# Key products and half of the value products of the third attention issued at the end of the expert stage before it

## The chip, the cores and the metric

The kernel runs on one core of one Trainium2 chip. The metric is the device time of one execution in microseconds (us). Five engines work from their own instruction queues and meet through semaphores: TensorE (PE; its weight loads are PEld), VectorE (DVE), ScalarE (ACT), GpSimd (POOL) and SyncE (SP), which issues most DMAs.

## The reference, cut to what matters

Four layers follow each other on a residual stream x of 16 x 64 tokens of 256 features; each adds a gated attention over a context and a gated feed-forward part. The change is at the border of the second layer's feed-forward part (eight experts, top 1) and the third layer's attention ("L2" in the reference, "a2" in the kernel):

```python
x = x + tanh(g_ffn[1]) * L1_ffn(layernorm(x), router_w, gate_w, up_w, down_w)
x = x + tanh(g_xattn[2]) * L2_xattn(layernorm(x), ctx_2048, mask, Wq, bq, Wk, bk, Wv, bv, Wo, qn_w, kn_w)
# L2_xattn: 16 query heads, 4 key/value heads, 128 features each
q = rmsnorm(h @ Wq + bq, qn_w);  k = rmsnorm(ctx @ Wk + bk, kn_w);  v = ctx @ Wv + bv
out = softmax(q @ k.T / sqrt(128) + mask) @ v;  x_add = out @ Wo
```

The keys and values come from the context, which is an input. They depend on nothing that the layers before compute.

## The kernel before, in words

Everything stays on the chip from the first load to the last store. The stages run one after the other: `m1_*` are the sorted experts, `a2_*` the attention after them, `m2_*` the next experts. Each engine has one function for each stage. At the end of a stage `finish(e, k)` raises `stage_done` and waits until all four compute engines have done so; SP waits for the same count before the loads of the next stage.

**Experts (`m1`).** The 1024 tokens are sorted by expert into 15 tiles. PE goes through the tiles (line 1724 is its last instruction, a small matmul that marks the end). DVE copies each output tile, SP stores it (line 1648), and then `a2_ahead` loads the key, value and query weights of the attention (lines 1952 and 1953) over the place of the expert weights. After all 15 tiles are stored, POOL gathers the rows back (line 1880) in token order, DVE adds them to x (line 1867), and the stage ends.

**Attention (`a2`).** DVE computes the layer norm of x. PE turns the context tokens and then the normed tokens (`tokens_turned`, line 1971, 16 transposes each), ACT copies them from PSUM (line 2099) over two tiles that the program names `ctxT_yT_hi` and `ctxT_yT_lo`. Then come slots n = -7 to 39, which every engine goes through in the same written order. The 8 tiles of tokens are called pairs (two batches in one tile); a pair takes four slots, and each pair has two units w of eight heads. In a slot PE has, in this order and as far as they fall due:

- the scores of unit w (line 1984, n = 2w), the transposes of probabilities (line 1992, n = 2w + 3), and heads times values (`heads_out`, line 2004, n = 2w + 5)
- the transposes of normed keys (`keys_turned`, line 2013, n = 4i - 1)
- the key product of pair i (`key_or_value(i, 0)`, line 2027, n = 4i - 3) or the value product (`key_or_value(i, 1)`, n = 4i + 3), both into PSUM bank 4, 128x512 in f32: two calls that the trace shows as four instructions
- sums of query squares (line 2059) together with the output product (line 2065)
- the next query product (`queries`, line 2037), into bank 6

The keys of a pair go through DVE (`keys_biased`, line 2193, adds the bias from PSUM), ACT (squares, line 2130), DVE (sums, lines 2199 and 2200), POOL (power of minus a half, line 2259), DVE (`keys_normed`, line 2207) and back to PE (line 2013) within two slots. `queries` on DVE (line 2163) frees bank 6 for the next query product. `outT` on DVE (line 2185) copies what `heads_out` made, as two copies of 128x512. After the last unit DVE makes the layer norm of tiles 0 to 6 (`ln_tiles`) and only then the last residual (line 2222).

The two lines on which all order rests are

```python
e.wait_ge(stage_done, 4 * k)
for n in A2_SLOTS:
```

Of the kernel before, what the change touches and what calls it, by code (L numbers as in the profile page):

```python
# [18 lines left out]
F32 = mybir.dt.float32  # L19
# [61 lines left out]
def program(nc, a):  # L81

    ctx = ExitStack()
    with ctx:
# [197 lines left out]
        def setup_pool(e):  # L282
# [3 lines left out]
        A2_TOTALS = dict(weights_loaded=48, wo_loaded=16, tables_loaded=80, tokens_in_psum=8, tokens_ready=8,  # L286
                         q_in_psum=32, q_squared=32, q_read=0, q_ready=32, squares_in_psum=32, squares_read=8, q_rstd_ready=8,
                         k_in_psum=8, k_squared=8, k_read=8, k_sums_ready=8, k_rstd_ready=8, k_normed=8, kT_in_psum=8, kT_ready=8,
                         v_in_psum=8, v_ready=8, scores_in_psum=16, scores_read=16, max_ready=16, exp_ready=16, sums_ready=16, probs_ready=16,
# [1361 lines left out]
        def m1_pe(e):  # L1651
# [72 lines left out]
            finish(e, 5, e.matmul(ps[:, 0, 0:1], identb[:, :], identb[:, 0:1], start=True, stop=True))  # L1724

        def m1_act(e):
# [39 lines left out]
            finish(e, 5)  # L1766
# [128 lines left out]
        m = Map(nc, ARENA, END - 24 * 1024)  # L1895
        a2wo = m("a2_wo", [P, HQ, D], F32)
        a2kt = m("a2_kT", [P, 2, HK, P], F32)
        a2v = m("a2_v", [P, 2, HK, HD], F32)
# [9 lines left out]
        a2row = m("a2_bias_rows", [P, 2, 512], F32)  # L1908
# [9 lines left out]
        def a2_over(name, shape, dt, offset):  # L1918
            return nc.alloc_sbuf_tensor_at("a2_" + name, shape, dt, offset=offset)
        a2wkv = a2_over("wk_wv", [P, 2, KC, HK * HD], F32, END - 24 * 1024)  # L1920
        a2wq = a2_over("wq", [P, KC, HQ * HD], F32, END - 16 * 1024)
        a2tok = [t[:, :, :, :].rearrange("p r k n -> p (r k n)").bitcast(F32).rearrange("p (r n) -> p r n", r=2) for t in (YCh, YCl)]

        a2_w, a2_wo, a2_in = a2_sem("weights_loaded"), a2_sem("wo_loaded"), a2_sem("tables_loaded")
# [23 lines left out]
        def a2_ahead(e):  # L1948

            e.wait_ge(*m1_dn.at(TILES))  # L1950
            for r, name in enumerate(("a2_wk", "a2_wv")):
                e.dma_start(a2wkv[:, r, :, :], a[name].rearrange("(c p) n -> p c n", p=P)).then_inc(a2_w.sem, 16)
            e.dma_start(a2wq[:, :, :], a["a2_wq"].rearrange("(c p) n -> p c n", p=P)).then_inc(a2_w.sem, 16)

        def a2_sync(e):
            e.wait_ge(stage_done, 20)
            e.dma_start(a2c[:, 0:20], a["a2_cols"]).then_inc(a2_in.sem, 16)
            for r, name in enumerate(("a2_bk", "a2_bv")):
                e.dma_start(a2row[:, r, :], a[name].unsqueeze(0).broadcast_to([P, 512])).then_inc(a2_in.sem, 16)
# [3 lines left out]

        def a2_pe(e):
            def tokens_turned(src, r):
                for b in range(4):
                    cc, th = b % 2, b // 2
                    for j in range(4):
# [1038 lines left out]
```

## Time and profile before

| what | value |
|---|---|
| three runs | 1503.03, 1507.39, 1508.20 us (median 1507.39) |
| the profiled execution | 1499.09 us, its span 1497.3 us |
| PE busy over the span | 1205.3 us (81%) |
| DVE, ACT, POOL busy | 867.8, 607.0, 323.5 us |
| mean granted TensorE clock | 0.873 of full speed |
| PE idle between experts and attention | 603.10 to 618.85 us |
| attention, first query product to end | 629.60 to 867.3 us |

The profiled execution is one run of the program, and all times of engines are from its span's start. A granted clock of 1.00 is 2.4 GHz and one of 0.50 is 1.2 GHz; a number between is a mean over a stretch. An engine's idle time matters only where nothing else holds the end.

### The profile page before, as it was taken

The page shows a single profiled execution, that of the slowest core. Times are in us where ns is not written, and L with a number is a line of the kernel's source. Part 1 is how long each engine was busy: PE and PEld are TensorE (multiplying, and loading weights), DVE is VectorE, ACT ScalarE, POOL GpSimd, SP SyncE. Part 2 cuts the span into 40 slices and gives each one's busy share as a digit, 9 for nine tenths or more (in the row PEclk, how much of TensorE's full clock was granted, in tenths as well). Part 3 has the DMA queues.
Part 4 walks back from the last instruction along what each step waited for, and adds up shares of the span by engine and source line. Part 5 has one row for each costly group of instructions (what it writes and reads, how often), then busy time and mean ns, then how long its engine had stood idle before and what let it go on. Part 6 is the DMA issues. An engine that isn't in the chain of part 4 may idle for free.

```text
span 1497.3 us, 23300 instructions
## 1 busy us (share of the span) xinstructions
PE 1205.3 (81%) x8532; PEld 858.6 (57%) x8577; DVE 867.8 (58%) x1843; ACT 607.0 (41%) x1323; POOL 323.5 (22%) x261
## 2 busy tenths in 40 slices
PE   1573674888885499489999936999997899999986
PEld 1352453444433266488888733555556688888854
DVE  6678795677774463334544575333335776656476
ACT  2441351555563131133333222433333665656443
POOL 1312001111100100221221102445440332222322
PEclk7555796799995699799999957999997999999998
DMA  7100006100002220500000051111103000000010
GB/s 237 51 2 1 0 1 265 65 2 2 2 1 102 81 78 36 195 1 1 1 1 1 1 182 32 43 53 42 42 0 119 0 1 1 1 1 1 1 43 28
DMA packets 32307, 64.31 MB, mean 43 GB/s; under 512 B 5361, under 2 KB 23281, under 8 KB 30289
## 3 DMA queue, kind: packets, MB, share of 16 engines
q1 hardware_dynamic: 31440, 60.90, 11.4%
q0 software_dynamic: 768, 2.10, 0.4%
q8 instruction: 62, 1.02, 0.3%
q14 instruction: 37, 0.30, 0.1%
HBM read 55.26 MB, written 9.70 MB: 43 GB/s over the span
## 4 chain that ended last, share of the span: by engine, by line
PE 50%; issue 19%; DVE 14%; POOL 4%; ACT 3%; DMA 1%; DVEq 0%; SPq 0%; POOLq 0%; ACTq 0%
PE psum L1401 8%; PE psum L1383 4%; PE psum L2420 4%; PE psum L2448 4%; PE psum L2410 4%; PE psum L2392 2%; PE psum L2374 2%; PE psum L1069 2%; PE psum L1043 2%; PE psum L2746 2%; PE psum L1011 1%; PE psum L1076 1%; POOL a_q_rstd L2265 1%; DVE ln_stats L163 1%; PE psum L2037 1%
## 5 line engine op out<-in xcount | busy, mean ns | idle before, releaser
L1468 DVE TENSOR_TENSOR m_silu_up<-psum,m_silu 128x512 f32<-128x512 f32 x50 | 34.6, 691 | 133.3 <-PE psum L1401 133.3
L1135 ACT ACTIVATE c_probs<-psum 128x512 f32<-128x512 f32 x128 | 76.3, 598 | 66.0 <-PE psum L1054 66.0
L1239 DVE TENSOR_REDUCE c_max<-psum 128x2 f32<-128x512 f32 x128 | 84.4, 687 | 27.0 <-PE psum L1043 20.5
L1401 PE MATMUL psum<-ctxT_yT_hi,m_w_lo 128*128 128x512 bf16 x200 | 76.5, 382 | 8.5 <-DVEq L1460 7.2
L1401 PE MATMUL psum<-ctxT_yT_lo,m_w_hi 128*128 128x512 bf16 x200 | 76.3, 382 | 0.0
L2448 PE MATMUL psum<-a_wo,a_outT 128*128 128x256 f32 x256 | 75.1, 405 | 0.7 <-DVE x_tok L2629 0.7
L1496 POOL TENSOR_TENSOR m_h_lo<-m_h,m_h_hi 128x512 bf16<-128x512 f32 x50 | 57.9, 1158 | 82.0 <-ACT m_h_hi L1440 82.0
L2065 PE MATMUL psum<-a_wo,a_outT 128*128 128x256 f32 x256 | 75.2, 407 | 0.0
L1440 ACT ACTIVATE m_h_hi<-m_h 128x512 bf16<-128x512 f32 x50 | 31.5, 630 | 90.5 <-DVE m_h L1473 90.5
L1401 PE MATMUL psum<-ctxT_yT_hi,m_w_hi 128*128 128x512 bf16 x175 | 66.8, 382 | 0.0
L1252 POOL TENSOR_TENSOR c_rope_terms<-c_rope_terms 128x256 f32<-128x256 f32 x16 | 11.6, 726 | 254.3 <-DVE c_rope_terms L1195 254.3
L2163 DVE TENSOR_TENSOR a_qT<-psum,a_columns 128x512 f32<-128x512 f32 x32 | 22.0, 689 | 75.3 <-PE psum L2037 75.3
L1353 POOL TENSOR_TENSOR m_w_lo<-m_w,m_w_hi 128x768 bf16<-128x768 f32 x27 | 44.4, 1646 | 85.1 <-ACT m_w_hi L1347 85.1
L2123 ACT ACTIVATE a_probs<-a_probs,a_max 128x64 f32<-128x64 f32 x128 | 42.7, 334 | 47.3 <-DVE a_max L2177 47.3
L2420 PE MATMUL psum<-ctxT_yT_hi,a_wq 128*128 128x128 f32 x256 | 53.0, 290 | 7.7 <-DVE a_q_cos L2585 7.0
L1689 PE MATMUL psum<-m_w,m_tileT 128*128 x120 | 56.9, 619 | 2.3 <-DVE m_tileT L1844 2.3
L2571 DVE TENSOR_REDUCE a_max<-psum 128x4 f32<-128x512 f32 x32 | 22.1, 691 | 63.2 <-PE psum L2374 63.0
L2488 ACT ACTIVATE a_q_squares<-psum 128x512 f32<-128x512 f32 x32 | 19.1, 598 | 93.9 <-PE psum L2420 93.9
L2512 ACT ACTIVATE a_probs<-psum,a_max,a_q_rstd 128x128 f32<-128x128 f32 x128 | 56.8, 459 | 0.1
L2105 ACT ACTIVATE a_q_squares<-a_qT 128x512 f32<-128x512 f32 x32 | 20.1, 629 | 87.8 <-DVE a_qT L2163 87.5
L1433 ACT ACTIVATE m_silu<-psum 128x512 f32<-128x512 f32 x50 | 29.8, 596 | 62.3 <-PE psum L1401 62.3
L1383 PE MATMUL psum<-m_w_hi,m_h_hi 128*128 128x256 bf16 x200 | 54.5, 272 | 0.6 <-POOL m_h_lo L1496 0.6
(482 smaller groups left out, 3513.5 us busy)
## 6 DMA issues: line engine op xcount, KB each, us to landing
m_w<-m_w SPq DMA_DIRECT2D x8, 1536.0 KB, 17.1
m_w<-m_w SPq DMA_DIRECT2D x27, 384.0 KB, 3.0
a_wq<-a_wq SPq DMA_DIRECT2D x2, 2048.0 KB
a_wo<-a_wo SPq DMA_DIRECT2D x2, 2048.0 KB, 12.5
a_trig<-trig_sin_cos SPq DMA_DIRECT2D x1, 2048.0 KB, 6.2
ctxT_yT_hi<-f_gate_up SPq DMA_DIRECT2D x2, 1024.0 KB, 6.6
a_sin_cos<-a_trig SPq DMA_DIRECT2D x1, 2048.0 KB, 10.1
m_rows<-m_zeros SPq DMA_DIRECT2D x1, 1920.0 KB, 13.9
```

The costliest lines, as they stand in the source:

```text
L1135: e.activation(c1P[:, n % 8, :, :], ps[:, 2 + n % 2, :].rearrange("p (k t) -> p k t", k=2), ACT.Exp, scale=float(1.0 / np.sqrt(np.float32( ...
L1239: e.tensor_reduce(c1M[:, u % 2, j, :], ps[:, c1_score_bank(n), :].rearrange("p (q t) -> p q t", q=2), AX.X, ALU.max).then_inc(c1_mx, 1)
L1353: e.tensor_tensor(wl[:, s, :], wr[:, s, :], wh[:, s, :], ALU.subtract).then_inc(s_wl, 1)
L1383: ins = e.matmul(o, l[:, b, t], r[:, s, 2 * D:3 * D], start=(first and i % 2 == 0 and x == 0), stop=False, skip_group_check=True)
L1401: ins = e.matmul(ps[:, bank, :], l[:, s, o + kc * P:o + (kc + 1) * P], r[:, kc, tk], start=(x == 0), stop=(x == 3 * KC - 1))
L1496: e.tensor_tensor(hl[:, n_ % hb, :], hf[:, n_ % hb, :], hh[:, n_ % hb, :], ALU.subtract).then_inc(s_hl, 1)
L1689: ins = e.matmul(ps[:, 1 + 2 * r + t % 2, :], m1xT[:, t % 2, kc, :], m1w[:, bass.ds(own + (2 * r + kc) * 512, 512)], start=(kc == 0), stop ...
L2065: ins = e.matmul(ps[:, 7, 0:D], a2at[:, i % 2, h, :, :], a2wo[:, h, :], start=(h == 0 and g is None), stop=(h == HQ - 1), skip_group_check ...
L2410: ins = e.matmul(ps[:, 4 + r, :], a3tok[kk][:, b, :, :], a3wkv[:, r, kk, :], start=(kk == 0), stop=(kk == KC - 1))
L2420: ins = e.matmul(out[:, :, h, :], a3wq[:, kk, (4 * j + h) * HD:(4 * j + h + 1) * HD], a3tok[kk][:, 2 * i:2 * i + 2, 1, :], start=(kk == 0) ...
L2448: ins = e.matmul(ps[:, 7, 0:D], a3at[:, i % 2, h, :, :], a3wo[:, h, :], start=(h == 0 and g is None), stop=(h == HQ - 1), skip_group_check ...
L2512: ins = e.activation(a3sc[:, u % 3, p_ * P:(p_ + 1) * P], ps[:, u % 2, p_ * P:(p_ + 1) * P], ACT.Exp, bias=a3mx[:, u % 3, p_:p_ + 1], scal ...
```

## The change

The turning of the context tokens, all eight key products and the value products of pairs 0 to 3 are taken out of the slots. PE and ACT do them at the end of their `m1` functions, after they have raised `stage_done` and before they wait for the others. ACT now copies the products from PSUM without the bias, to two new tiles, `a2_k_raw` and a value tile for all eight pairs. The key bias is added by DVE from that copy. The value bias is no longer added to the values; `outT` adds it (a row of probabilities sums to one) as four operations of 128x256 in place of two copies. The value products of pairs 4 to 7 stay in their slots. The loads keep their place in SP's queue; one bias row less is loaded.

```diff
-        def finish(eng, k, last=None):
+        def done(eng, last=None):
...
             eng.sem_inc(stage_done, 1)
+
+        def finish(eng, k, last=None):
+
+            done(eng, last)
             eng.wait_ge(stage_done, 4 * k)
...
-            finish(e, 5, e.matmul(ps[:, 0, 0:1], identb[:, :], identb[:, 0:1], start=True, stop=True))
+            done(e, e.matmul(ps[:, 0, 0:1], identb[:, :], identb[:, 0:1], start=True, stop=True))
+            context_pe(e)
+            e.wait_ge(stage_done, 20)
...
-            finish(e, 5)
+            done(e)
+            e.wait_ge(f3_q, 3)
+            context_act(e)
+            e.wait_ge(stage_done, 20)
...
+        def a2_context_pe(e):
+            a2_tokens_turned(e, ct, 0)
+            e.wait_ge(*a2_x.at(4))
+            e.wait_ge(*a2_kvw.at(32))
+            for x in range(NT + A2_EARLY_V):
+                i, r = x % NT, x // NT
+                if x >= 4:
+                    e.wait_ge(a2_cr, x - 3)
+                for kk in range(KC):
+                    ins = e.matmul(ps[:, x % 4, :], a2tok[kk][:, 0, i * P:(i + 1) * P], a2wkv[:, r, kk, :], start=(kk == 0), stop=(kk == KC - 1))
+                ins.then_inc(a2_kp.sem, 1)
+
+        def a2_context_act(e):
+            a2_tokens_copied(e, 0)
+            for x in range(NT + A2_EARLY_V):
+                i, r = x % NT, x // NT
+                own = a2v[:, i, :, :].rearrange("p j d -> p (j d)") if r else a2kw[:, i, :]
+                e.wait_ge(*a2_kp.at(x + 1))
+                e.activation(own, ps[:, x % 4, :], ACT.Copy).then_inc(a2_cr, 1)
...
-            tokens_turned(ct, 0)
-            tokens_turned(yt, 1)
+            a2_tokens_turned(e, yt, 1)
             e.wait_ge(*a2_x.at(8))
-            e.wait_ge(*a2_w.at(48))
+            e.wait_ge(*a2_w.at(16))
+            e.wait_ge(a2_cr, NT + A2_EARLY_V)
...
-                if a2_pair(n, 3) is not None:
-                    key_or_value(a2_pair(n, 3), 0)
-                if a2_pair(n, -3) is not None:
-                    key_or_value(a2_pair(n, -3), 1)
+                if a2_pair(n, -3) is not None and a2_pair(n, -3) >= A2_EARLY_V:
+                    value(a2_pair(n, -3))
...
                 for b2 in range(2):
-                    ins = e.tensor_copy(a2at[:, i % 2, 8 * hb:8 * hb + 8, b2, :], ps[:, 1 + 2 * b2, :].rearrange("p (h t) -> p h t", h=8))
+                    for j in range(2):
+                        h = 8 * hb + 4 * j
+                        ins = e.tensor_scalar(a2at[:, i % 2, h:h + 4, b2, :],
+                                              ps[:, 1 + 2 * b2, j * 256:(j + 1) * 256].rearrange("p (h t) -> p h t", h=4),
+                                              a2c[:, 20 + 2 * hb + j:21 + 2 * hb + j], None, ALU.add)
...
-                e.tensor_tensor(a2kf[:, :], ps[:, 4, :], a2row[:, 0, :], ALU.add).then_inc(a2_kr.sem, 1)
+                e.tensor_tensor(a2kf[:, :], a2kw[:, i, :], a2row[:, :], ALU.add).then_inc(a2_kr.sem, 1)
```

Where the instructions stand now. PE at the border of the two stages, before: the last down product of the experts, the marker, the context and the normed tokens turned, then the first query product.

```order
L1707 MATMUL psum<-m_w,m_hT 128x256
L1724 MATMUL psum<-ident_bf 128x1
L1971 MATMUL psum<-ident_f,ctx_tok 128x128 x16
L1971 MATMUL psum<-ident_f,y_tok 128x128 x16
L2037 MATMUL psum<-ctxT_yT_hi,a_wq 128x2x64
```

The same place of PE in the changed kernel; the pair of rows of line 2000 stands there twelve times.

```order
L1712 MATMUL psum<-m_w,m_hT 128x256
L1729 MATMUL psum<-ident_bf 128x1
L1982 MATMUL psum<-ident_f,ctx_tok 128x128 x16
L2000 MATMUL psum<-a_wk_wv,ctxT_yT_hi 128x512
L2000 MATMUL psum<-a_wk_wv,ctxT_yT_lo 128x512
...
L1982 MATMUL psum<-ident_f,y_tok 128x128 x16
L2069 MATMUL psum<-ctxT_yT_hi,a_wq 128x2x64
```

The twelve products have moved ahead of the transposes of the normed tokens, and the context's transposes ahead of the barrier. ACT at the same border, before: the last two copies of turned expert rows, then the copies of turned tokens, four for the context and four for the normed tokens.

```order
L1754 ACTIVATE m_hT<-psum 128x512 x2
L2099 ACTIVATE ctxT_yT_hi<-psum 128x512
L2099 ACTIVATE ctxT_yT_lo<-psum 128x512
L2099 ACTIVATE ctxT_yT_hi<-psum 128x512
L2099 ACTIVATE ctxT_yT_lo<-psum 128x512
L2099 ACTIVATE ctxT_yT_hi<-psum 128x512
L2099 ACTIVATE ctxT_yT_lo<-psum 128x512
L2099 ACTIVATE ctxT_yT_hi<-psum 128x512
L2099 ACTIVATE ctxT_yT_lo<-psum 128x512
L2105 ACTIVATE a_q_squares<-a_qT 128x512 x5
```

ACT there in the changed kernel:

```order
L1761 ACTIVATE m_hT<-psum 128x512 x2
L1989 ACTIVATE ctxT_yT_hi<-psum 128x512
L1989 ACTIVATE ctxT_yT_lo<-psum 128x512
L1989 ACTIVATE ctxT_yT_hi<-psum 128x512
L1989 ACTIVATE ctxT_yT_lo<-psum 128x512
L2009 ACTIVATE a_k_raw<-psum 128x512 x8
L2009 ACTIVATE a_v<-psum 128x512 x4
L1989 ACTIVATE ctxT_yT_hi<-psum 128x512
L1989 ACTIVATE ctxT_yT_lo<-psum 128x512
L1989 ACTIVATE ctxT_yT_hi<-psum 128x512
L1989 ACTIVATE ctxT_yT_lo<-psum 128x512
L2131 ACTIVATE a_q_squares<-a_qT 128x512 x5
```

The copies of the twelve products stand ahead of the four copies of normed tokens. DVE in slot n = 5, before: the query copy, the inverted sums, `outT`, the biased keys of pair 2, and the query copy of slot 6.

```order
L2163 TENSOR_TENSOR a_qT<-psum,a_columns 128x512
L2218 RECIPROCAL a_sums<-a_sums 128x8
L2185 COPY a_outT<-psum 128x8x64 x2
L2193 TENSOR_TENSOR a_k_biased<-psum,a_bias_rows 128x512
L2163 TENSOR_TENSOR a_qT<-psum,a_columns 128x512
```

DVE in that slot in the changed kernel:

```order
L2189 TENSOR_TENSOR a_qT<-psum,a_columns 128x512
L2246 RECIPROCAL a_sums<-a_sums 128x8
L2213 TENSOR_SCALAR a_outT<-psum,a_columns 128x4x64 x4
L2223 TENSOR_TENSOR a_k_biased<-a_k_raw,a_bias_row 128x512
L2189 TENSOR_TENSOR a_qT<-psum,a_columns 128x512
```

The order of DVE is the same; `outT` has four operations in place of two, and the keys are read from the copy.

## Rows read from the trace of the kernel before

**Rows 1.** Who waited for whom, PE, 629 to 868 us: total, times, longest.

```profile
PE psum L2013 <- DVE a_k L2207: 5.5, 4, 2.0
PE psum L2037 <- DVE a_qT L2163: 0.9, 1, 0.9
```

**Rows 2.** Groups by line, 629 to 868 us: busy us, mean ns, idle before.

```profile
L2027 PE MATMUL psum<-a_wk_wv,ctxT_yT_hi 128*128 128x512 f32 x32 | 17.1, 616 | 0.0
```

**Rows 3.** Timeline, PE, the first key product: start, duration.

```profile
640.06 1.02 PE L2027 MATMUL psum<-a_wk_wv,ctxT_yT_hi 128*128 128x512 f32 x2
...
641.78 0.95 PE L2059 MATMUL psum<-ones_f,a_q_squares 128*128 128x1 f32 x8
```

**Rows 4.** Timeline, the border of the two stages.

```profile
602.93 0.17 PE L1724 MATMUL psum<-ident_bf 128*128 128x1 bf16 x1
618.85 3.32 PE L1971 MATMUL psum<-ident_f,ctx_tok 128*128 128x128 f32 x16 [15.75 <-DVEq L136]
625.20 3.72 PE L1971 MATMUL psum<-ident_f,y_tok 128*128 128x128 f32 x16 [3.03 <-DVE y_tok L171]
628.38 0.60 ACT L2099 ACTIVATE ctxT_yT_hi<-psum 128x512 f32<-128x512 f32 x1 [0.26 <-PE psum L1971]
628.95 0.60 ACT L2099 ACTIVATE ctxT_yT_lo<-psum 128x512 f32<-128x512 f32 x1
629.60 0.49 PE L2037 MATMUL psum<-ctxT_yT_hi,a_wq 128*128 128x128 f32 x2 [0.69 <-ACT ctxT_yT_lo L2099]
```

**Rows 5.** Windows: length, busy of PE, PEld, DVE, ACT, POOL, PE clock, DMA share, GB/s.

```profile
604.80:605.20 0.40, 0.00 (x0) 0.00 (x0) 0.00 (x0) 0.00 (x0) 0.00 (x0) 1.00 0.13 36
603.00:610.00 7.00, 0.10 (x2) 0.00 (x0) 0.42 (x1) 0.00 (x0) 3.58 (x4) 0.86 0.77 275
610.00:618.00 8.00, 0.00 (x0) 0.00 (x0) 2.64 (x7) 0.00 (x0) 4.04 (x5) 0.50 0.76 303
618.00:623.00 5.00, 3.32 (x16) 3.08 (x16) 4.64 (x22) 2.29 (x4) 0.11 (x1) 0.63 0.42 121
625.00:630.00 5.00, 4.12 (x19) 3.47 (x20) 2.52 (x9) 2.36 (x4) 0.00 (x0) 0.66 0.91 314
750.00:800.00 50.00, 50.00 (x352) 43.95 (x351) 21.57 (x39) 15.76 (x61) 8.18 (x7) 1.00 0.00 1
475.00:480.00 5.00, 3.80 (x18) 3.70 (x18) 0.86 (x4) 0.51 (x2) 0.00 (x0) 0.50 0.00 0
```

**Rows 6.** Timeline, SP's issues and POOL's first gather.

```profile
604.42 0.51 SPq L1952 DMA_DIRECT2D a_wk_wv<-a_wv  x1
605.51 0.98 POOL L1880 DMA_INDIRECT m_rows_back<-m_back,m_slot  x1 [109.89 <-DMA m_back<-m_rows_by_expert]
```

**Rows 7.** DMA packets in 608.4 to 608.6 us and in 608.8 to 609 us.

```profile
DMA packets 27, 0.11 MB, mean 553 GB/s; under 512 B 9, under 2 KB 9, under 8 KB 15
DMA packets 7, 0.06 MB, mean 287 GB/s; under 512 B 0, under 2 KB 0, under 8 KB 0
```

**Rows 8.** Timeline, slot n = 11: keys normed on DVE, PE up to their transposes.

```profile
717.62 0.60 PE L1992 MATMUL psum<-ident_f,a_probs 128*128 128x128 f32 x4
717.62 0.69 DVE L2207 TENSOR_TENSOR a_k<-a_k_biased,a_k_rstd 128x512 f32<-128x512 f32 x1 [1.12 <-POOL a_k_rstd L2259]
718.15 1.13 PE L2004 MATMUL psum<-a_probsT,a_v 64*128 64x256 f32 x8
719.21 0.65 PE L2013 MATMUL psum<-ident_f,a_k 128*128 128x128 f32 x4
```

**Rows 9.** Timeline, one expert copy of 128x256, and the attention's end.

```profile
603.13 0.42 DVE L1848 COPY m_rows_by_expert<-psum 128x256 f32<-128x256 f32 x1 [1.30 <-PE psum L1707]
857.82 7.17 PE L2065 MATMUL psum<-a_wo,a_outT 128*128 128x256 f32 x32
857.93 1.29 DVE L2185 COPY a_outT<-psum 128x512 f32<-128x512 f32 x2 [0.59 <-PE psum L2004]
...
866.84 0.47 DVE L2222 SCALAR_TENSOR_TENSOR x_tok<-psum,gates,x_tok 128x256 f32<-128x256 f32 x1
```

More of the change, by code:

```diff
@@ L1962, in a2_sync, with a2_tokens_turned, a2_tokens_copied @@
             e.dma_start(a2wo[:, :, :], a["a2_wo"].rearrange("(h p) n -> p h n", p=P)).then_inc(a2_wo.sem, 16)
-        def a2_pe(e):
[L1965 to L1968, printed above, removed]
-                        if r:
-                            e.wait_ge(y_ready, 4 * NT + 4 * th + j + 1)
-                        ins = e.transpose(ps[:, 4 * r + b, j * P:(j + 1) * P], src[:, 4 * th + j, cc * P:(cc + 1) * P], identf[:, :])
-                    ins.then_inc(a2_xp.sem, 1)
+        def a2_tokens_turned(e, src, r):
+            for b in range(4):
+                cc, th = b % 2, b // 2
+                for j in range(4):
+                    if r:
+                        e.wait_ge(y_ready, 4 * NT + 4 * th + j + 1)
+                    ins = e.transpose(ps[:, 4 * r + b, j * P:(j + 1) * P], src[:, 4 * th + j, cc * P:(cc + 1) * P], identf[:, :])
+                ins.then_inc(a2_xp.sem, 1)
+        def a2_tokens_copied(e, r):
+            for b in range(4):
+                cc, th = b % 2, b // 2
+                e.wait_ge(*a2_xp.at(4 * r + b + 1))
+                e.activation(a2tok[cc][:, r, th * HALF:(th + 1) * HALF], ps[:, 4 * r + b, :], ACT.Copy).then_inc(a2_x.sem, 1)
+        def a2_context_pe(e):
[16 more added lines that the diff above has]
+                e.activation(own, ps[:, x % 4, :], ACT.Copy).then_inc(a2_cr, 1)
+        def a2_pe(e):
             def scores(w):
@@ L2014, in keys_turned, with value @@
                 ins.then_inc(a2_kTp.sem, 1)
[L2016 to L2025 removed]
+            def value(i):
+                if i > A2_EARLY_V:
+                    e.wait_ge(*a2_vr.at(i - A2_EARLY_V))
                 for kk in range(KC):
[L2027 to L2028 removed]
+                    ins = e.matmul(ps[:, 4, :], a2tok[kk][:, 0, i * P:(i + 1) * P], a2wkv[:, 1, kk, :], start=(kk == 0), stop=(kk == KC - 1))
+                ins.then_inc(a2_vp.sem, 1)
             def queries(g):
@@ L2094, in a2_act @@
         def a2_act(e):
-            for r in range(2):
-                for b in range(4):
-                    cc, th = b % 2, b // 2
-                    e.wait_ge(*a2_xp.at(4 * r + b + 1))
-                    e.activation(a2tok[cc][:, r, th * HALF:(th + 1) * HALF], ps[:, 4 * r + b, :], ACT.Copy).then_inc(a2_x.sem, 1)
+            a2_tokens_copied(e, 1)
             def query_squares(g):
@@ L2210, in values @@
             def values(i):
[L2211 to L2214 removed]
+                e.wait_ge(*a2_vp.at(i - A2_EARLY_V + 1))
+                e.tensor_copy(a2v[:, i, :, :].rearrange("p j d -> p (j d)"), ps[:, 4, :]).then_inc(a2_vr.sem, 1)
             def inverted_sums(w):
@@ L2233, in a2_dve @@
                     queries(n + A2_AHEAD - 1)
-                if a2_pair(n, -4) is not None:
+                if a2_pair(n, -4) is not None and a2_pair(n, -4) >= A2_EARLY_V:
                     values(a2_pair(n, -4))
```

61 lines of the change are left out of this document (25 added, 36 removed).

## The prediction

> **What bounds the kernel now.** I read three views, in this order. The page gives PE busy for 81% of the span, which says little of one stage, so I went to the view of waits for the attention alone. There PE waits 5.5 us for normed keys (four times, 2.0 at most) and 0.9 us for a query copy [rows 1]; two more waits stand at the stage's two ends. Over 239 us that is all that PE is idle for long, and in 750 to 800 us it is busy for the whole 50 at a clock of 1.00 [rows 5]. So inside the slots the end is set by the sum of PE's work, and a microsecond less on PE is a microsecond less.
>
> The border before it is bound otherwise. PE's last instruction of the experts is over at 603.10 and its next starts at 618.85 [rows 4]: the time is that of the stores, POOL's gather and DVE's sum. From 618.85 to 625.2 DVE makes the layer norm, and the context's transposes (3.32 us) lie beside it. The normed tokens are turned from 625.20, ACT's last copy starts at 628.95, and the first query product at 629.60 [rows 4]. The window in which moved work is free is therefore 603.1 to 625.2 on PE, 22.1 us, less the time in which it can't run.
>
> **The change part by part.**
>
> *Removed from the slots.* One product takes 640.06 to 641.78, 1.72 us [rows 3]. The sixteen products are 64 instructions of line 2027; half of them stand in [rows 2], with a mean of 616 ns, four of which would be 2.5 us. They overlap at their ends, so the spacing is what PE spends. Twelve products are 20.6 us. In steady slots other PE work closes up behind them. I looked for what could be late next.
>
> - Keys: DVE ends `keys_normed` at 718.31, and PE comes to the transposes at 719.21 [rows 8]: 0.9 us to spare. That chain starts with the scores of the slot before, and neither of the two slots loses a product ahead of the transposes. It moves with PE, so the spare time stays, and the waits of 5.5 us stay too. Cost nothing; if this cover failed, see the rivals.
> - Query copies: in two slots of the run-up (n = -3 and n = 1) the key product was the long piece between two query products. Left is the squares' piece, 0.79 us by the spacing of eight (their 0.95 in [rows 3] has a tail). The wait with nothing between was 0.9 [rows 1], so 0.1 is left, twice: +0.2.
> - Value bias: DVE adds it in `outT`, and no longer in the value step, which stays as a copy for four pairs.
>
> *`outT`.* Two copies take 1.29 us [rows 9]. The nearest row for one of the four new operations is a copy of 128x256 from PSUM, 0.42 us [rows 9], so 1.68 at most and 1.29 at least; I take 1.7. It is +0.4 us on DVE, sixteen times. In the slots DVE is busy for less than half of the time (21.57 of 50 us [rows 5]), and PE asks for the result two slots later: nothing. At the end it is on the path: DVE ends the last `outT` at 859.2, goes through the layer norm of seven tiles and starts the last residual at 866.84, while PE's product is over at 864.99 (857.82 + 7.17) [rows 9]. So once +0.4 (0 to 0.4).
>
> *Moved to the border.* PE needs the turned context and both weights.
>
> - Transposes: four take 0.53 us at full clock, by the start of the next piece [rows 8], so 16 take 2.1: 603.2 to 605.3. ACT needs 0.57 for a copy by the spacing of two [rows 4], and is through soon after 606. Both have ended before the weights come.
> - Weights: the loads are issued by 604.93 [rows 6], and nobody waited for them before. They are moved in packets of 2 KB, and the query weights behind them in 8 KB. Between 608.4 and 608.6 fifteen of 27 packets are below 8 KB, nine of them small ones; between 608.8 and 609 none [rows 7]. So the last of them moves at about 608.7. From the last packet to the start of whoever waits I have one row: the last expert tile's store has mostly moved by 604.8, with 36 GB/s left in 604.8 to 605.2 [rows 5], and POOL, which waits for it, starts at 605.51 [rows 6]. So I add 0.5, and the first product starts at 609.2. Earliest is 608.8; latest is the end of all this traffic, about 615.5, if the semaphore came only with the query weights (DVE's sum of the gathered rows is under way in 610 to 618, so the gathers behind the same traffic have ended by then [rows 5]).
> - The Trainium skill, DMA: Bandwidth & Descriptors, section "Anatomy of one DMA", puts a fixed cost of about 2 us on a DMA and says that most of it is the wait for the write receipt after the data. By that figure, counted from the last packet, the first product would start at 610.7 and the sum would be 1.5 us worse. No row here shows such a gap.
> - Clock: PE is idle from 605.3. After its work ended at 603.1 before, the mean clock of 603 to 610 was 0.86, so it fell to 1.2 GHz at 608.0, and stayed there to 618 [rows 5]. When the transposes began at 618.85 it came back after 2.8 us (0.63 in 618 to 623), and after 625.2 in 3.3 us (0.66 in 625 to 630) [rows 5]. So the first 2.8 to 3.3 us of the products run at half speed, which loses half of that, 1.5 us. Bounds: 0 if the transposes of 603 to 605 keep the clock up, 2.8 if it stays low for twice the shorter of the two, 5.6 us.
> - End of the products: 609.2 + 20.6 + 1.5 = 631.3. This is past 625.2, so they are only partly covered. Four PSUM banks are used in turn and ACT's copy is a third of a product: no wait there.
> - Then the normed tokens. PE turns them at full clock, 0.53 us a bank. ACT first ends its last product copy (+0.65), then makes four copies at 0.57: 2.9 us after the products. First query product at 634.3, against 629.60: **+4.7 us**.
>
> The layer norm, the gather and SP's loads don't wait for PE or ACT, since both raise `stage_done` before the new work. The table loads behind the barrier are one row fewer and long landed by 634.
>
> *Sum.* -20.6 + 0.2 + 0.4 + 4.7 = **-15.3 us**. The profiled execution took 1499.1 us, so it would take 1483.8. Its time lies 8.3 us below the median of the three runs shown, 1507.4. The change is the same for both, so against the median it is **1492.1 us**, 1.0% less.
>
> **The rivals.**
>
> 1. *The weights come late.* If the semaphore comes only when the traffic ends (615.5), the first query product is at 615.5 + 20.6 + 1.5 + 2.9 = 640.5, 10.9 late, and the sum -9.1: 1498.3. For it: loads of one queue and the gathers share the engines. Against it: the packets of 2 KB are done almost seven microseconds earlier [rows 7].
> 2. *The key chain takes over.* If what is taken from slots n = 4i - 3 comes back as a wait for normed keys, the eight key products (13.8 us) give nothing: -1.5, 1505.9, no change. For it: PE already waits 5.5 us there in the first pairs [rows 1], and has only 0.9 to spare later [rows 8]. Against it: the chain's start is the scores of slot 4i - 2, behind the removed work. It would take DVE or ACT to be late at the start of that slot, and DVE is half idle.
> 3. *The clock stays low under the products: slower.* At 1.2 GHz twelve products take 41.3 us and end at 650.5. The normed tokens then take 3.3 us to turn [rows 4] and 0.65 for the last copy, and the first query is at 654.5, 24.9 late: +4.9 us, 1512.3. It turns the gain into a loss from 33.8 us of low clock on: the products may end 20.0 - 2.9 = 17.1 after 629.6, at 646.7, which is 16.9 past 609.2 + 20.6. For it: at 475 to 480 PE was busy for 3.80 of 5 us and the clock still 0.50 [rows 5]. Against it: the products leave no gaps, and both starts after 618 brought it back in about 3 us.
> 4. *It doesn't move.* ACT could be held at the border by its new wait for the third group of ternary weights. PE turns parts of that group in the expert tiles before, so it is ready when PE is done, and I give it nothing.
>
> **How the numbers follow.** My forecast gets 0.74; its own range is 1489.7 (weights at 608.8, no low clock, `outT` free: -17.7) to 1493.4 (5.6 us of low clock: -14.0). Rival 1 gets 0.08, rival 2 0.09, rival 3 0.04, and 0.05 is left for what I haven't seen, both ways. The three runs before lie up to 4.4 us from their median, so I widen by about 4.5 on either side and take in rival 1: 1485 to 1500. A change of 0.5%, 7.5 us, is about what a measurement of this kernel can tell from none. Faster by more: the forecast, rival 1 and a part of the rest, 0.84. Within: rival 2, rival 3 (+0.3%) and a part of the rest, 0.13. Slower by more: 0.03.
>
> **What the changed profile would show.** Line 2000 on PE starts at 609 to 610 (right) or near 615 (rival 1); its rows are spaced 0.43 us after some 3 us, or 0.86 for all (rival 3). The first query product (line 2069) stands near 634. From there to the last residual, the attention is 237.7 - 20.0 = 217.7 us long. PE's waits for normed keys sum to about 5.5 again; with rival 2 they are near 19. I would be wrong most easily in where the products end, since each microsecond of lateness there is one of the gain, and next in the slots, if a wait for DVE shows that the trace of before hides.

## The result, and the profile after

| | before | changed |
|---|---|---|
| four runs each | 1503.03, 1507.39, 1508.20, 1509.36 us | 1482.05, 1484.27, 1484.38, 1485.53 us |
| median | 1507.8 us | 1484.33 us |
| the profiled execution (span) | 1499.09 us (1497.3) | 1482.05 us (1480.3) |

The ratio of the times is 0.9848 with a 95% interval of 0.9823 to 0.9873: 1.5% faster in this comparison. I had forecast 1492.1 us and a range down to 1485, so the direction was right, and the time lies 0.7 us below the range. Over all the runs further down (93 of the kernel before, 16 of the changed one) the gain is 1.1%. The interval above doesn't reach down to it, since all four runs of the kernel before happened to be long ones. One run of those below (filled_wait, 1505.14 us) is a slow one, over 1.5% above the fastest of its kernel, and stands in no ratio, median or mean.

The timeline of PE in the changed kernel at the border (start, duration, idle time before and its releaser in brackets), which answers to [rows 4] and [rows 3]:

```profile
599.46 0.17 PE L1729 MATMUL psum<-ident_bf 128*128 128x1 bf16 x1
599.80 1.94 PE L1982 MATMUL psum<-ident_f,ctx_tok 128*128 128x128 f32 x16 [0.18 <-PE psum L1729]
606.83 2.04 PE L2000 MATMUL psum<-a_wk_wv,ctxT_yT_hi 128*128 128x512 f32 x2 [5.09 <-DMA a_wk_wv<-a_wv]
608.67 1.91 PE L2000 MATMUL psum<-a_wk_wv,ctxT_yT_lo 128*128 128x512 f32 x2
610.38 1.33 PE L2000 MATMUL psum<-a_wk_wv,ctxT_yT_hi 128*128 128x512 f32 x2
611.54 1.02 PE L2000 MATMUL psum<-a_wk_wv,ctxT_yT_lo 128*128 128x512 f32 x2
...
628.71 1.02 PE L2000 MATMUL psum<-a_wk_wv,ctxT_yT_lo 128*128 128x512 f32 x2
629.57 1.91 PE L1982 MATMUL psum<-ident_f,y_tok 128*128 128x128 f32 x16
632.38 0.49 PE L2069 MATMUL psum<-ctxT_yT_hi,a_wq 128*128 128x128 f32 x2 [0.90 <-ACT ctxT_yT_lo L1989]
```

The gap of 15.75 us on PE is gone. Left of it are 5.09 us in which PE waits for the value weights. The products end at 629.57, long after the layer norm (its first operation stands at 616.02), so the end of the border is set by them, as forecast. Each row above is two of the product's four instructions. The rows are spaced 1.84, 1.71 and 1.16 us at first and 0.86 after that: the clock was low for about 4 us.

The waits of PE in 600 to 860 us (total, times, longest), which answer to [rows 1]:

```profile
PE psum L2052 <- DVE a_k L2237: 5.5, 4, 2.0
PE psum L2000 <- DMA a_wk_wv<-a_wv: 5.1, 1, 5.1
...
PE psum L2069 <- ACT ctxT_yT_lo L1989: 0.9, 1, 0.9
PE psum L2069 <- DVE a_qT L2189: 0.9, 1, 0.9
```

The wait for normed keys is 5.5 us as before; no wait took the place of what left the slots. But the windows (length, busy PE, PEld, DVE, ACT, POOL, PE clock, DMA share, GB/s) show something that no view of waits has:

```profile
646.00:650.00 4.00, 2.68 (x22) 2.41 (x21) 1.52 (x4) 1.15 (x2) 1.04 (x1) 1.00 0.00 0
650.00:652.00 2.00, 1.34 (x13) 1.34 (x13) 1.28 (x3) 0.68 (x2) 1.23 (x1) 0.99 0.00 0
652.00:655.40 3.40, 3.40 (x17) 3.40 (x18) 0.00 (x0) 0.52 (x1) 1.68 (x1) 0.51 0.00 0
655.40:658.00 2.60, 2.60 (x26) 2.60 (x25) 1.30 (x2) 1.60 (x2) 0.00 (x0) 1.00 0.00 0
660.00:700.00 40.00, 37.30 (x312) 35.42 (x312) 22.12 (x47) 21.39 (x92) 12.28 (x8) 1.00 0.01 2
```

PE's first wait for normed keys, 2.0 us long, ends at 650.66. From 652.0 to 655.4 the clock is 1.2 GHz, and then it is back. PE is busy for all of that time, so the whole loss is on the path.

The end of the attention, which answers to [rows 9]:

```profile
841.96 7.17 PE L2097 MATMUL psum<-a_wo,a_outT 128*128 128x256 f32 x32
842.08 1.66 DVE L2213 TENSOR_SCALAR a_outT<-psum,a_columns 128x256 f32<-128x256 f32 x4 [0.59 <-PE psum L2043]
843.65 2.38 DVE L167 BATCH_NORM_STATS2 ln_stats<-x_tok 128x6 f32<-128x256 f32 x7
...
851.36 0.48 DVE L2250 SCALAR_TENSOR_TENSOR x_tok<-psum,gates,x_tok 128x256 f32<-128x256 f32 x1
```

`outT` takes 1.66 us as four operations, 1.29 before, and the layer norm begins right behind it.

**Where the time went.** To keep apart what the change does from what differs between executions, I measure from the marker (the last PE instruction of the experts) in each profile. The first five columns are us from the marker's start, to the start of the work named, and for the attention's end to the end of the last residual. That fifth column is called the stretch below. The profiled executions of the runs below are in it too.

| profile | first product | normed tokens turned | first query product | first keys turned | attention's end | keys turned to end |
|---|---|---|---|---|---|---|
| before | – | 22.27 | 26.67 | 46.50 | 264.38 | 217.88 |
| before_again | – | 22.38 | 26.80 | 46.63 | 264.52 | 217.89 |
| before_fourth | – | 22.28 | 26.76 | 46.60 | 264.51 | 217.91 |
| before_third | – | 22.44 | 27.13 | 50.37 | 269.91 | 219.54 |
| out_bias_only | – | 22.45 | 26.91 | 46.74 | 265.02 | 218.28 |
| before_filled | – | 23.58 | 27.35 | 47.19 | 266.73 | 219.54 |
| changed | 7.37 | 30.11 | 32.92 | 51.20 | 252.38 | 201.18 |
| after_again | 6.84 | 30.22 | 33.03 | 51.31 | 252.47 | 201.16 |
| after_third | 7.05 | 29.98 | 32.80 | 51.08 | 252.25 | 201.17 |
| ev0_keys_only | 6.75 | 23.09 | 26.18 | 44.45 | 252.47 | 208.02 |
| ev8_all_values | 6.87 | 36.84 | 39.65 | 57.92 | 252.31 | 194.39 |
| filled_wait | 7.24 | 27.91 | 30.72 | 49.00 | 248.53 | 199.53 |
| filled_both | 7.23 | 27.91 | 30.72 | 49.00 | 248.55 | 199.55 |
| filled_again | 6.57 | 27.24 | 30.06 | 48.34 | 249.50 | 201.16 |

From the marker to the attention's end the change gives 264.38 - 252.38 = 12.0 us, where I had 15.3. The profiled executions differ by 17.0. Of the rest, 3.5 us lie ahead of the marker (602.93 and 599.46) and 1.5 behind the attention (span less end: 1497.3 - 867.31 = 630.0, and 1480.3 - 851.84 = 628.5). The change touches nothing there. Most of the 3.5 is a spell of low clock in a stage long before. The windows of the kernel before there:

```profile
448.00:452.00 4.00, 2.94 (x26) 1.18 (x26) 3.67 (x19) 2.72 (x6) 0.00 (x0) 0.87 0.00 0
452.00:456.00 4.00, 2.36 (x13) 0.45 (x9) 3.66 (x17) 1.96 (x4) 0.00 (x0) 0.50 0.03 6
456.00:460.00 4.00, 3.50 (x26) 1.14 (x26) 0.35 (x2) 0.77 (x2) 0.00 (x0) 0.50 0.00 0
```

and of the changed kernel, with the same instructions:

```profile
448.00:452.00 4.00, 2.94 (x31) 1.21 (x30) 3.67 (x19) 2.72 (x6) 0.00 (x0) 1.00 0.00 0
452.00:456.00 4.00, 2.01 (x21) 0.66 (x20) 3.66 (x17) 2.24 (x5) 0.00 (x0) 1.00 0.02 6
456.00:460.00 4.00, 1.30 (x11) 0.65 (x12) 2.50 (x3) 0.49 (x2) 0.00 (x0) 1.00 0.00 0
```

The layer norm that follows there starts at 464.8 before and at 461.6 after, 3.2 us. This is chance and not the change: in before_again and before_fourth the clock is 1.00 in 452 to 456, and in after_third, a profile of the changed kernel, it is 0.50 there.

### The profile page after: what moved, and what is told of

Same layout as the page of the kernel before. It is cut to its first block, busy times and chain, and to the rows that moved or that the text cites. A ratio compares the mean times of both kernels' runs of the same rounds, so it can differ in the third digit from the quotient of the medians.

```text
span 1480.3 us, 23367 instructions
## 1 busy us (share of the span) xinstructions
PE 1204.7 (81%) x8577; PEld 853.3 (58%) x8577; DVE 871.6 (59%) x1871; ACT 613.4 (41%) x1335; POOL 323.5 (22%) x261
## 4 chain that ended last, share of the span: by engine, by line
PE 56%; DVE 16%; issue 10%; POOL 3%; ACT 3%; DMA 1%; DVEq 0%; SPq 0%; POOLq 0%; ACTq 0%
PE psum L1406 9%; PE psum L1388 4%; PE psum L2448 4%; PE psum L2476 4%; PE psum L2438 4%; PE psum L1694 3%; PE psum L2420 2%; PE psum L2402 2%; PE psum L2774 2%; PE psum L1048 2%; PE psum L2000 2%; PE psum L1712 2%; PE psum L1074 1%; PE psum L1016 1%; PE psum L2069 1%
## 5 line engine op out<-in xcount | busy, mean ns | idle before, releaser
L1244 DVE TENSOR_REDUCE c_max<-psum 128x2 f32<-128x512 f32 x128 | 84.3, 687 | 24.8 <-PE psum L1048 18.4
L1406 PE MATMUL psum<-ctxT_yT_hi,m_w_hi 128*128 128x512 bf16 x200 | 76.8, 384 | 6.8 <-DVEq L1465 6.8
L1388 PE MATMUL psum<-m_w_lo,m_h_hi 128*128 128x256 bf16 x200 | 54.4, 272 | 0.0
```

The lines of the kernel that those rows point to most:

```text
L1244: e.tensor_reduce(c1M[:, u % 2, j, :], ps[:, c1_score_bank(n), :].rearrange("p (q t) -> p q t", q=2), AX.X, ALU.max).then_inc(c1_mx, 1)
L1388: ins = e.matmul(o, l[:, b, t], r[:, s, 2 * D:3 * D], start=(first and i % 2 == 0 and x == 0), stop=False, skip_group_check=True)
L1406: ins = e.matmul(ps[:, bank, :], l[:, s, o + kc * P:o + (kc + 1) * P], r[:, kc, tk], start=(x == 0), stop=(x == 3 * KC - 1))
```

## The experiments

The times of runs are from three chips. On each the kernels ran together with the kernel before (35 runs, median 1496.16; 17 runs, 1504.09; 23 runs, 1507.49), and a ratio is to these runs. What a change does to the attention is read from the table above, since runs of one kernel differ by more than most of these edits bring.

### Each kernel once more

**before_again**, the kernel before, unchanged.

> The kernel before once more, unchanged, for a second profile and for the spread. The two profiled executions so far differ by 17.0 us of span, of which 12.0 lie between the end of the experts and the end of the attention; 3.4 lie ahead and the rest behind, in stages that the change does not touch, and the medians differ by 23.5. Theory 'chance of the clock': what lies outside varies from one execution to the next, since the granted clock falls and rises at other places. Then the window 448 to 468 us of this profile may show the clock at 1.00 where it was 0.50, the last layer norm of the stage before the experts may stand anywhere from 461 to 465 us, and the ratio to the kernel before is 1.00 with an interval of about 0.3%. Theory 'systematic': outside of the border and the attention this profile repeats the first one of before within 0.5 us in each stage.

Measured: 1499.88 us (12 runs, 1493.97 to 1507.67), ratio 1.0019 (0.9984 to 1.0053), and a stretch of 264.52 us. Theory 'chance of the clock' holds: the clock is 1.00 in 452 to 460, and the layer norm starts at 462.7, between the 464.8 and 461.6 of the first two profiles. What lies ahead of the marker is chance too. The marker stands at 597.9 to 602.9 in four profiles of the kernel before and at 599.5 to 604.0 in three of the changed one, so the 3.5 us of the first pair of profiles are no gain.

**after_again**, the changed kernel, unchanged.

> The changed kernel once more, unchanged, for its spread. 47 runs of the unchanged kernel in the last session fell into two groups, 31 from 1492.9 to 1501.6 and 16 from 1503 to 1510, and the first three timed runs of before (1503, 1507, 1508) were all of the upper one. Theory 'two groups, and the change is worth 12': the lower groups are 12 apart, this kernel runs at 1482 to 1487 two times in three, and has an upper group of its own near 1495; the ratio over both groups is about 0.992. Theory 'the change also removes the upper group': no run above 1490, and a ratio of 0.988 or less. Theory '23 us as first measured': 0.985.

Measured: 1487.15 us (6 runs, 1483.83 to 1491.23), ratio 0.9892 (0.9854 to 0.9931), stretch 252.47. The counts in this expectation were wrong: of the 47 runs that I had then, 29 were in the lower and 18 in the upper group. Nearest comes the theory that the change also removes the upper group, though one run (1491.23) is above its 1490.

**before_third** (one run) and **after_third**, both unchanged.

> The kernel before for one more profile. If this execution is of the upper group (1503 and above), the stage in which it loses 12 us against the other profiles shows a lower granted clock while PE is busy; if it is of the lower group, it repeats them.

> The changed kernel for a third time, beside the kernel before and the two filled ones on one chip. From marker to the end of the attention 252.4 us as in both profiles so far. Over 69 runs of before (mean 1501.4) and 10 of this (mean 1485.9) the difference is 15.5. Theory 'stage and clock': 1484 to 1489 in most runs, a mean of 1486 to 1487, few above 1492. Theory 'luck in 10 runs': a share of a third to a half at 1494 to 1498, and a mean difference of 12.

before_third took 1497.61 us, with a stretch of 269.91, 5.4 longer than the others. after_third took 1486.44 us (6 runs, 1485.15 to 1490.65), ratio 0.9899 (0.9852 to 0.9946), stretch 252.25, as theory 'stage and clock' said. Windows of before_third, two at the border and two in the slots:

```profile
619.00:625.00 6.00, 4.00 (x16) 3.18 (x16) 3.48 (x14) 2.39 (x4) 0.00 (x0) 0.50 0.93 317
625.00:630.00 5.00, 4.13 (x17) 3.84 (x18) 0.69 (x1) 0.38 (x1) 0.00 (x0) 0.50 0.02 6
...
646.00:650.00 4.00, 2.02 (x19) 1.83 (x18) 1.61 (x5) 1.09 (x2) 2.69 (x2) 1.00 0.00 0
650.00:654.00 4.00, 4.00 (x24) 4.00 (x23) 0.69 (x1) 0.65 (x2) 1.27 (x1) 0.57 0.02 4
```

Here the clock stays at 1.2 GHz through the transposes of the normed tokens and into the query products (+3.4 us up to the first keys turned), and dips once more behind the first wait for keys (+1.65). The kernel before can lose 5 us at this border that it doesn't lose in other executions. In its three profiles the changed kernel has one and the same length, within 0.2 us.

**before_fourth**, the kernel before (one run).

> The kernel before for one more profile. The stretch from marker to the end of the attention is 264.4 or about 270, by where the clock falls. If the execution takes 1503 or more, its profile shows in which stage the upper group loses its 12 us.

Measured: 1496.67 us, stretch 264.51. It isn't of the upper group, so it doesn't show where that group loses its time.

### How many value products are moved

**ev0_keys_only** moves no value product, **ev8_all_values** all eight.

```diff
-A2_EARLY_V = 4
+A2_EARLY_V = 0     # and 8 in the other kernel
```

> The changed kernel with no value product moved: eight products at the border and all eight value products in their slots. Theory 'cover': only what lies beside the gather and the layer norm is a gain. The products end 6.9 us earlier, near 622.7 us, about when the first normed tokens are ready, so the first query product comes 6 to 6.9 us earlier than in the changed kernel and the slots are 6.9 longer: 1484 to 1486, no difference to the changed kernel. Theory 'each product counts': 1.72 us lost for each of four, 1491.

> The changed kernel with all eight value products moved as well: sixteen products at the border. Theory 'cover': four more products end 6.9 us later, the first query product comes 6.9 later, and the slots are 6.9 shorter: 1484, no difference to the changed kernel. Theory 'each product counts': 1477. A third possibility is that PE, with no product left in the slots, waits for DVE in the last pairs: 1486 to 1490, with waits of PE on DVE beyond pair 3.

Measured: 1488.53 us (12 runs, 1484.15 to 1493.94), ratio 0.9929 (0.9898 to 0.9960) with none, and 1485.86 us (12 runs, 1481.28 to 1494.46), 0.9926 (0.9899 to 0.9953) with all. The stretch is 252.47, 252.38 and 252.31 us for none, four and all eight. From none to all, the first query product comes 13.47 us later (39.65 - 26.18) and the rest after the first keys is 13.63 us shorter (208.02 - 194.39): 1.7 us a product both times. So the whole gain comes from the eight key products, which lie beside the stores, the gather and the layer norm. The run times alone would not say so: 1488.5 with none lies between the two theories (1484 to 1486, and 1491), and only the 1485.9 with all speaks against 'each product counts' (1477). With keys only, the normed tokens are turned at 23.09, 0.7 us after the layer norm would have let them: the cover is just used up. The four value products of the change are neither gain nor loss. With all eight moved PE has no new wait for DVE, so the third possibility is out too.

### The value bias in `outT` alone

**out_bias_only**: the kernel before, with `outT` as the change has it and the value step as a plain copy.

```diff
-                    ins = e.tensor_copy(a2at[:, i % 2, 8 * hb:8 * hb + 8, b2, :], ...)
+                    for j in range(2):
+                        ins = e.tensor_scalar(a2at[:, i % 2, h:h + 4, b2, :], ..., a2c[:, 20 + 2 * hb + j:21 + 2 * hb + j], None, ALU.add)
...
-                e.tensor_tensor(a2v[:, i % 2, :, :]..., ps[:, 4, :], a2row[:, 1, :], ALU.add)
+                e.tensor_copy(a2v[:, i % 2, :, :]..., ps[:, 4, :])
```

The line of the bias columns is left out here: their load is four columns wider, as in the change.

> The kernel before with one part of the change: the value bias is added in the copy of head outputs, as four operations of 128x256 in place of two copies of 128x512, and no product is moved. My reckoning: four operations take 1.66 us in place of 1.29; the slots hide it, and at the end of the attention DVE is on the path, so +0.4 us: no difference that a comparison can tell, and in the trace the layer norm behind the last of them starts 0.4 us later after PE's last heads-times-values piece. Rival: DVE is late in the slots, 16 times 0.4: +6 us, and PE waits for DVE in steady slots.

Measured: 1502.48 us (12 runs, 1496.14 to 1506.05), ratio 0.9987 (0.9958 to 1.0016), and the stretch from the first keys 218.28 against 217.89: +0.4 us. That is the term of the prediction. PE's waits for normed keys are 5.5 us as before, and no wait for `outT` stands in the view, so the rival (+6 us) is out.

### Is the low clock what the wait costs?

**filled_wait**: the changed kernel, with 40 transposes of context tokens into a PSUM bank that nobody reads, behind the context's transposes, so that PE is busy while it waits for the weights.

```diff
             a2_tokens_turned(e, ct, 0)
+            for j in range(40):
+                e.transpose(ps[:, 5, (j % 4) * P:(j % 4 + 1) * P], ct[:, j % 8, 0:P], identf[:, :])
             e.wait_ge(*a2_x.at(4))
```

> The changed kernel with 40 more transposes of context tokens into an idle PSUM bank, 4.9 us of PE in the 5.1 us in which it waits for the weights; their results are not used. Theory 'clock': the products no longer start at 1.2 GHz, twelve take 20.7 us in place of 22.7, and the first query product comes 2.0 us earlier: 1482.3, with the clock at 1.00 throughout the products. Theory 'the clock is worth nothing here': 1484.3, the same. If the additional work is late itself, up to 0.3 us more.

The timeline of PE, and windows up to and behind the first wait for keys:

```profile
601.57 4.53 PE L1994 MATMUL psum<-ident_f,ctx_tok 128*128 128x128 f32 x40
606.69 1.10 PE L2002 MATMUL psum<-a_wk_wv,ctxT_yT_hi 128*128 128x512 f32 x2 [0.59 <-DMA a_wk_wv<-a_wv]
607.62 1.02 PE L2002 MATMUL psum<-a_wk_wv,ctxT_yT_lo 128*128 128x512 f32 x2
```

```profile
606.80:612.00 5.20, 5.20 (x13) 2.33 (x14) 0.00 (x0) 1.19 (x2) 3.78 (x4) 1.00 1.01 418
...
649.00:653.00 4.00, 4.00 (x38) 4.00 (x38) 0.77 (x2) 1.66 (x3) 2.47 (x1) 1.00 0.00 0
```

The products run at 1.00 from the first one and take 20.67 us in place of 22.74; the clock doesn't dip behind the wait for keys, which is 2.0 us long as before. The stretch is 248.53 us, 3.85 less. So the cost of the low clock is shown: 2.1 us in the products, 1.65 in the slots. The runs don't follow: their median is 1492.19 us (11 runs, 1478.78 to 1497.41), ratio 0.9937 (0.9898 to 0.9976), where theory 'clock' said 1482.3. The profiled execution was the fastest of them.

**filled_both**: as filled_wait, and 15 more such transposes ahead of each of the first two turns of keys, so that the waits there are filled too.

```diff
+                if i < 2:
+                    for j in range(15):
+                        e.transpose(ps[:, 1, (j % 4) * P:(j % 4 + 1) * P], ct[:, j % 8, 0:P], identf[:, :])
```

> The kernel with the filled wait, and with 15 more transposes ahead of the transposes of keys of pairs 0 and 1, where PE waits 2.0 and 1.9 us for normed keys; results unused. In the profiles of the changed kernel, of keys only and of all values the granted clock fell behind the first of these waits (0.69 in 650 to 655, where PE was idle for 2.0 us just before); with the filled wait alone it did not. Theory 'clock in the slots': no clock below 1.00 from the first product to the end of the attention in this profile, and 1.8 us less than the changed kernel in those executions that have the dip, so 3.8 us less with the filled wait: 1480.5 where the changed kernel has 1484.3. Theory 'chance alone': the dip is still there at times, and nothing is gained over the filled wait.

Measured: 1485.31 us (6 runs, 1478.30 to 1487.85), ratio 0.9870 (0.9830 to 0.9910). The waits for keys fall from 5.5 to 2.3 us, the clock is 1.00 from the first product to the attention's end, and the stretch stays at 248.55, as in the first profile of filled_wait, which had no dip either. The mean of the runs is 3.2 us below that of after_again on the same chip (1483.9 and 1487.1), near the 3.8 of theory 'clock in the slots'. With six runs each the two intervals overlap, so this gain is not shown.

**filled_again**, the kernel of filled_wait once more.

> The changed kernel with 40 more transposes in the wait for the weights, again, since its 12 runs were spread from 1478.8 to 1505.1. From marker to the end of the attention 248.5 us, 3.9 less than the changed kernel, as in its first profile and in the one with both waits filled. Theory 'stage and clock': mean 3 to 4 us under after_third. Rival 'given back elsewhere': the stretch is short, but the mean over runs is not below that of the changed kernel, since other stages take it back.

Measured: 1491.56 us (12 runs, 1479.40 to 1500.87), ratio 0.9921 (0.9885 to 0.9957). The window behind its first wait for keys:

```profile
651.00:655.00 4.00, 4.00 (x24) 4.00 (x24) 0.51 (x1) 0.35 (x1) 1.50 (x1) 0.61 0.00 0
```

This time the dip is there (201.16 us from the first keys, 1.65 more), behind the same fill and the same wait of 2.0 us. So the filling at the border makes the products fast both times, and the dip in the slots is there in one of two profiles of one kernel. Over 23 runs of this kernel the mean is 1490.2 us, against 1486.3 over 16 of the changed one, though its stretch is 2.8 to 3.9 us shorter. What is won in the attention is lost elsewhere in many executions, as the rival said, and I have no profile of one of those. Their mean granted clock is lower: 0.868 to 0.878 in the runs above 1490 us, 0.880 to 0.889 in the five below 1482.

**before_filled**: the kernel before, with 120 such transposes behind the marker and 30 between the two groups of turned tokens.

```diff
+            for j in range(120):
+                e.transpose(ps[:, 5, (j % 4) * P:(j % 4 + 1) * P], ct[:, j % 8, 0:P], identf[:, :])
+            e.wait_ge(stage_done, 20)
...
             tokens_turned(ct, 0)
+            for j in range(30):
+                e.transpose(ps[:, 5, (j % 4) * P:(j % 4 + 1) * P], ct[:, j % 8, 0:P], identf[:, :])
             tokens_turned(yt, 1)
```

> The kernel before, no product moved, with transposes of context tokens into an idle PSUM bank wherever PE waits at the border: 120 behind the marker of the experts (13.6 us of the 15.8) and 30 between the transposes of context and of normed tokens (3.4 of 3.3 us); results unused. In four profiled executions of before the stretch from the marker to the end of the attention took 264.4, 264.5, 265.0 (with the value bias moved) and 269.9 us; the long one had the clock at 1.2 GHz into the first query products and again behind the first wait for keys. Theory 'border clock': with the clock kept up the stretch takes 263.5 to 264.5, never 270, and the mean of the runs is 2 to 3 us under that of before. Theory 'this is the upper group': no run above 1503 either. Rival: the upper group has its cause in other stages, and a third to a half of the runs stay above 1503.

Measured: 1501.15 us (12 runs, 1495.83 to 1505.68), ratio 0.9986 (0.9956 to 1.0016), stretch 266.73. The clock is at 1.00 all over the border, and still the first query product comes 0.7 us later, since the barrier opens 1.3 us later (17.27 us after the marker, 15.96 before), and the slots have the dip of 1.65. Theory 'border clock' (263.5 to 264.5, never more) is wrong. No run is above 1505.68, where 14 of the 23 runs of the kernel before on that chip lie, but three are above 1503 and none is below 1495. Keeping the clock up at the border isn't what makes the changed kernel faster: without the move of the products it brings nothing.

## Why the prediction missed, point by point

**The mechanism was right.** Eight key products run beside the stores, the gather and the layer norm; PE's work sets the end of the slots; no wait for keys took their place (rival 2: 5.5 us as before), the weights came early (rival 1: first product at 606.83, not near 615), the clock was low for the first products only (rival 3: rows of two instructions 0.86 us apart from the fourth row on).

**Products out of the slots, -20.6, and the query waits, +0.2: right.** Up to the first keys turned, one product less and one query wait shorten the way from the first query product by 1.55 us (19.83 and 18.28); I had 1.72 - 0.2. Without a dip of the clock it takes 217.81 us from the first query product to the end (filled_wait, 248.53 - 30.72); the prediction said 217.7.

**`outT`, +0.4: right.** 1.66 us against 1.29, and +0.4 by itself in out_bias_only.

**The border, +4.7: too small, 6.25 measured** (32.92 - 26.67). Its parts:

- The first product comes 7.37 us after the marker; I had 609.2 - 602.93 = 6.3. What was wrong is when the packets of 2 KB end. I had read 608.7 from the trace of before, 5.8 us after its marker. In the changed kernel the last of them still moves at 606.2 to 606.3, 6.8 us after the marker. Its DMA packets in 606.2 to 606.3 and in 606.3 to 606.4 us are

```profile
DMA packets 8, 0.05 MB, mean 512 GB/s; under 512 B 1, under 2 KB 1, under 8 KB 2
DMA packets 2, 0.02 MB, mean 164 GB/s; under 512 B 0, under 2 KB 0, under 8 KB 0
```

  and the first product starts at 606.83, some 0.5 us behind. In the other profiles the last such packet ended 6.1 to 6.7 us after the marker and the products came at 6.57 to 7.24, again 0.5 us behind. So the 0.5 us from the last packet to the waiter was right. Why the packets end later than in the kernel before (5.7 to 6.0 there) was not tried.
- The Trainium skill, DMA: Bandwidth & Descriptors, section "Anatomy of one DMA", puts the fixed cost of a DMA on GpSimd's path at about 2 us, mostly the wait for the write receipt. Counted from the last packet it gave 610.7 for this start, 7.8 us after the marker. SP issued these loads, and all eight profiles show 0.5 us in place of 2.
- The clock cost 2.1 us in the products, not 1.5 (22.74 against 20.67 with the wait filled), still within my bounds of 0 to 2.8. Turning and copying the normed tokens took 2.81, where I had 2.9.

**What the sum didn't have: +1.65 in the slots.** The clock falls behind the first wait for normed keys. I had read these waits as 5.5 us that stay as they are. All three profiles of the changed kernel have the dip, and so do ev0_keys_only and ev8_all_values; three of the four of before don't, nor does out_bias_only. With it the slots give 16.7 us after the first keys (217.88 - 201.18) in place of 18.4. With 1.55 from the border and this, -15.3 becomes -12.1, and -12.0 was measured. Why the wait is followed by the dip in one kernel and mostly not in the other stays open.

**The step that failed is the last one of the sum: "The change is the same for both, so against the median it is 1492.1 us".** The terms together were 3.3 us too good, yet the time came out 7.8 us better than predicted. Runs of before fall into two groups: of 93 in all, 44 lie between 1492.86 and 1501.63 us (mean 1496.0) and 49 between 1502.89 and 1511.48 (mean 1507.5). The three runs known before the prediction, and all four of the comparison, are of the upper one, while the profiled execution, and so all rows that I summed, is of the lower. I took the 8.3 us between them as an offset that stays. The changed kernel has no upper group: 16 runs lie in 1482.05 to 1491.23, with a mean of 1486.3, and of the 24 runs with none or all of the value products moved none is above 1494.46. Its time is therefore to be set against the profile's own, 1499.09 - 12.0 = 1487.1, and not against the median. The 2.8 us from there to the 1484.33 of the comparison lie within the spread of the runs: the four of the comparison have a mean 2.2 us below that of all 16.

Two things here are luck. All four runs of before in the comparison were upper ones, which makes its gain 23.5 us where the means of all runs give 15.8 (1502.1 and 1486.3). And these 15.8 lie close to my 15.3 only because two errors cancel: the terms gave 3.3 us too much, and the upper group, which I didn't know of, adds to the mean of before. The profiled executions have a mean span of 1496.1 (four of before) and 1483.8 us (three of the changed kernel), 12.3 less, near the 12.0 of the stretch. Against the lower group alone the runs gain 9.7 us, against the upper one 21.3.

**What stays open.** No profile of a run of the upper group was caught (the four of before took 1496.67 to 1499.09 us), so where its 12 us lie isn't shown, nor why the change ends it. The runs give one hint. The mean granted clock is 0.865 to 0.877 in the upper runs (mean 0.870) and 0.876 to 0.885 in the lower ones (0.879); the changed kernel has 0.878 on average. But the first profiled execution of before has 0.873 in a span of 1497.3 us, and before_fourth 0.883 in 1494.9, so a low mean clock alone can come with 2.4 us as well, and it isn't shown to be the cause. It isn't the value bias alone: six of the 12 runs of out_bias_only are above 1502.5. That the low clock at the border of the kernel before is a part of it is an argument only: before_third shows that 5.4 us can be lost there in one execution, which itself took 1497.61 us, and before_filled, whose profile has none of that loss, has no run above 1505.68 but a mean of 1501.1. Nor is it shown what the filled kernels lose in their long runs.

## What to carry to other kernels

Work that depends only on inputs belongs beside a barrier's DMA and gather time, up to the point where it fills that time; past it each further piece costs at the border what it saves later, so size the move by the cover and not by what can be moved (eight key products gave all of it here). Before you take a difference between two first profiles for a gain, profile each kernel again: 3.5 us ahead of the change were chance here. Before you add a difference to a median, ask whether the profiled execution belongs to the same group of runs as the median. A wait of 2 us on an engine that is the bound can cost nearly as much again in clock behind it (1.65 us here), and only the windows show it.

## What the runs showed of the hardware

- The granted clock of PE in one and the same part of the program differs between executions of one kernel: 0.50 (before) or 1.00 (before_again) in 452 to 456 us with the same instructions, 1.2 GHz into the query products or not (3.4 us), and a dip behind a wait of 2.0 us or none (1.65 us).
- From the last packet of the weights' load, issued by SP, to the start of the product that waits for it are 0.5 us, in all eight profiles with products at the border.
- The gathers landed later while PE was kept busy: issued at the same times after the marker, they let DVE's sum start 13.8 to 14.3 us after it in the four filled profiles and 12.4 to 13.1 in the others, and the barrier open at 17.3 to 17.8 and 16.0 to 16.6. Its cause was not tried.
- This program on one core has two groups of times 12 us apart (0.8%) for one kernel, on all three chips where it ran often (13 of 35, 11 of 17 and 16 of 23 runs in the upper one).
